# Self-attention of all batches as one stage, with its keys and queries in a ring, its sums turned by DMA, and the output projection in a second loop

## The reference

```
x   = L0(x, ctx_1024)                       # attention over 1601 rows of memory, a gate, RMS norm
n   = rms_norm(x, ln_in_w)
q,k,v = split(where(vm, n @ v_qkv, n @ l_qkv), 3)      # vm: which of two experts a token has
q,k = apply_rotary(heads(q,16,32), heads(k,16,32))
p   = softmax(causal(q * 32**-0.5 @ k.T))              # 16 heads, 512 x 512
ctx = p @ v
h   = x + where(vm, ctx @ v_dense, ctx @ l_dense)
h   = h + cross_attention(rms_norm(h), ctx_1024) @ cdense_w
out = h + where(vm, ffn_v(rms_norm(h)), ffn_l(rms_norm(h)))
```

## Time and profile before

| what | us |
| --- | --- |
| median of three runs | 2756.47 (2754.41 to 2765.78) |
| the profiled execution | 2762.2 |
| its span | 2760.1 |
| mean granted clock of TensorE | 0.863 of 2.4 GHz |
| the loop over batches, first product to the start of cross-attention | 39.3 to 1609.7 |

### The profile page before, as it was taken

The page is one execution under the profiler, slowest core; times in us unless marked ns, Lnnn a source line. Parts: engine busy times, 40 slices in busy tenths (PEclk is TensorE's granted clock), DMA queues, the critical chain, the costliest instruction groups (busy, mean ns, idle before and its releaser), DMA issues. The chain is left out here.

```text
span 2760.1 us, 35393 instructions
## 1 busy us (share of the span) xinstructions
PE 2270.3 (82%) x13534; PEld 1459.8 (53%) x13534; DVE 1598.8 (58%) x2420; ACT 937.4 (34%) x1627; POOL 394.5 (14%) x412
## 2 busy tenths in 40 slices
PE   5996776868758869659868649999999979999968
PEld 3673454654545745446634523444444357787846
DVE  4284433564423664442854458999999446666534
ACT  1131231221132212131312206888888822212101
POOL 0120001120002110002100000222222312221111
PEclk8986787976868967779868758999999989999989
DMA  4024044141062250261240392444444023343332
GB/s 151 24 75 101 13 96 157 47 106 48 16 165 85 66 132 3 70 179 31 77 107 1 83 171 44 82 82 82 82 85 91 15 83 91 102 115 86 100 84 72
DMA packets 196269, 227.89 MB, mean 83 GB/s; under 512 B 54134, under 2 KB 128250, under 8 KB 195306
## 3 DMA queue, kind: packets, MB, share of 16 engines
q1 hardware_dynamic: 189132, 217.98, 32.1%
q0 software_dynamic: 6656, 6.96, 1.0%
q10 hardware_dynamic: 288, 0.27, 0.0%
HBM read 162.76 MB, written 34.98 MB: 72 GB/s over the span
## 5 line engine op out<-in xcount | busy, mean ns | idle before, releaser
L1430 DVE TENSOR_REDUCE quarters<-ps 128x2 f32<-128x804 f32 x512 | 483.2, 991 | 52.4 <-PE ps L1464 50.8
L1395 ACT ACTIVATE pT_x<-ps 128x512 f32<-128x512 f32 (+1 forms) x832 | 451.6, 595 | 104.3 <-PE ps L1492 77.2
L184 DVE TENSOR_TENSOR w_lo<-w_raw,w_hi 128x512 fp32r<-128x512 f32 (+2 forms) x357 | 276.0, 773 | 12.2
L182 DVE CAST w_hi<-w_raw 128x512 fp32r<-128x512 f32 (+2 forms) x357 | 177.6, 498 | 181.9 <-PE ps L190 106.3
L1464 PE MATMUL ps<-kx_ring,qx_ring 63*128 63x402 f32 x1024 | 234.4, 470 | 45.7 <-DMA kx_ring<-cross_k_by_part 33.9
L1507 PE MATMUL ps<-pT_x,vx_ring 128*17 128x256 f32 (+1 forms) x3328 | 261.9, 388 | 0.2 <-ACT osb_x L1377 0.2
L1464 PEld LDWEIGHTS ps<-kx_ring,qx_ring 63*128 63x128 f32 x1024 | 100.4, 193 | 238.6 <-DVE quarters L1430 123.5
L877 ACT ACTIVATE pT_s<-ps 128x1024 f32<-128x1024 f32 (+3 forms) x128 | 88.8, 704 | 359.2 <-PE ps L963 359.2
L188 PE MATMUL ps<-mi_h,w_hi 128*128 128x512 f32 (+1 forms) x440 | 175.2, 398 | 37.4 <-issue 25.6
L894 DVE TENSOR_REDUCE row_max_s<-ps 128x1 f32<-128x128 f32 (+3 forms) x256 | 123.8, 491 | 137.9 <-PE ps L933 133.9
L1492 PE MATMUL ps<-qx_ring,kx_ring 64*128 64x512 f32 (+1 forms) x832 | 175.1, 417 | 6.2 <-ACT pT_x L1395 2.6
(11 more groups left out here) (273 smaller groups left out, 4512.3 us busy)
## 6 DMA issues: line engine op xcount, KB each, us to landing
kx_ring<-cross_k_by_part SPq DMA_DIRECT2D x96, 200.2 KB, 7.2
w_raw<-L_xattn_l_qkv SPq DMA_DIRECT2D x48, 256.0 KB, 3.0
w_raw<-L_xattn_v_qkv SPq DMA_DIRECT2D x48, 256.0 KB, 2.7
w_raw<-L_xattn_l_gate SPq DMA_DIRECT2D x40, 256.0 KB, 2.9
w_raw<-L_xattn_l_up SPq DMA_DIRECT2D x40, 256.0 KB, 2.9
w_raw<-L_xattn_l_down SPq DMA_DIRECT2D x40, 256.0 KB, 2.7
q_st<-early SPq DMA_DIRECT2D x32, 256.0 KB, 5.2
cross_v_by_group<-v_aug SPq DMA_DIRECT2D x16, 442.0 KB
```

The lines of the kernel that those rows point to most:

```text
L182: nc.vector.tensor_copy(hi, raw).then_inc(s_high, 1)
L184: nc.vector.tensor_tensor(out=lo, in0=raw, in1=hi.bitcast(f32), op=ALU.subtract).then_inc(s_split, 1)
L1395: nc.scalar.activation(pT[0:kn, u % 3, j, :], ps[0:kn, 5 + v % 3, :], ACT.Exp, scale=SCALE)\
L1430: nc.vector.tensor_reduce(out=quarters[:, g % 2, pair, :, q, quarter], in_=ps[:, at:at + 2, 0:MAXW], axis=AX.X, op=ALU.max)\
```

## The change

`gate_qkv` now stores the high and low parts of the queries and keys, the values, the stream `h` and the flag `early_v` to DRAM, and the first loop ends there. Then `self_attention` runs once, for 16 groups. SP loads each group into one of four slots of a ring, six DMAs of 32 partitions and one of values; the slot of group g is free for loading when the scores of group g-4 are done. A score product is one head and one key tile in one of three banks, each with its own exponential. The maxima have three banks too. The sums, their reciprocals and the shift go by way of DRAM with DMAs that POOL issues; POOL divides, and stores the rows. A second loop runs `add_projection`, which loads the rows, the two masks, the flag, the weights and `h` back, masks on DVE, rounds on ACT and subtracts on POOL, and then `cross_projections`.

```diff
+    qs_d, ks_d = scratch("self_q_by_part", [B, 2, D, S]), scratch("self_k_by_part", [B, 2, D, S])
+    vs_d = scratch("self_v_by_group", [B, NH // 4, P, ST, P])
+    att_d = scratch("self_rows_by_batch", [B, P, NH // 4, S])
+    gated_d = scratch("stream_after_gate", [B, P, DT, S])
+    early_d = scratch("early_v_by_batch", [B, 1, 1], i32)
     keep_d = scratch("keep_expert_by_token", [2, B, S])
...
+                                sp.dma_start(keep_d[:, b, :].rearrange("e (a n) -> a e n", a=1), keep_expert[0:1, :, :])\
+                                    .then_inc(s["s_up"], 16)
+                                sp.dma_start(early_d[b], early_v[:, :]).then_inc(s["s_up"], 16)
+                        sp.wait_ge(s["s_h"], DT)
+                        sp.dma_start(gated_d[b], h[:, :, :]).then_inc(s["s_up"], 16)
+                        for c in range(2 * DT):
+                            dst, k = qs_d if c < DT else ks_d, c % DT
+                            for part, rows, ready in ((0, hi, "s_rh"), (1, lo, "s_rl")):
+                                sp.wait_ge(s[ready], c + 1)
+                                sp.dma_start(dst[b, part, k * P:(k + 1) * P, :], rows[c].bitcast(f32)).then_inc(s["s_up"], 16)
+                        sp.wait_ge(s["s_vn"], ST)
+                        for g in range(NH // 4):
+                            sp.dma_start(vs_d[b, g], v_nat[:, :, g * P:(g + 1) * P]).then_inc(s["s_up"], 16)
+                        sp.wait_ge(s["s_up"], 16 * (3 + 4 * DT + NH // 4))
 
                     @block.scalar
...
             first = maxima + 1 + lead
-            start, queue, by_step = queue[:first], queue[first:], []
-            for u in range(groups * steps):
-                g, kt = divmod(u, steps)
-                now = [(("flip", "back")[kt], g - 1)] if kt < 2 and g else []
-                due = -(-(u + 1) * (maxima + 1) // steps)
-                while queue and len(start) + sum(o[0] in ("max", "turn") for d in by_step + [now] for o in d) < first + due:
-                    now.append(queue.pop(0))
+            start, feed, given, by_step = feed[:first], feed[first:], 0, []
+            for v in range(groups * steps):
+                g, i = divmod(v, steps)
+                now = [("flip", g - 1)] if g and i == 11 else []
+                due = -(-(v + 1) * (maxima + 1) // steps)
+                while feed and given < due:
+                    now.append(feed.pop(0))
+                    given += 1
                 by_step.append(now)
...
                 with nc.Block() as block:
                     @block.sync
                     def _(sp):
-                        stack_heads(sp, k_st, (late[0].bitcast(f32), late[1].bitcast(f32), late[0].bitcast(f32)), HALF, HALF, 0, s["s_late"])
-                        preload(sp, next_tiles, s_pre)
+                        sp.dma_start(k_r[STACK:STACK + 1, :, :].bitcast(f32).rearrange("a (r h) n -> a r (h n)", r=8),
+                                     ones_d[:, 0:RING * 4 // 8 * S].rearrange("(a r) n -> a r n", a=1)).then_inc(s["s_one"], 16)
                         for g in range(NG):
-                            sp.wait_ge(s["s_used"], place["turn", g] + 1)
+                            b, i, rows = g // GB, g % RING, slice(g % GB * P, (g % GB + 1) * P)
+                            if g >= RING:
+                                sp.wait_ge(s["s_sc"], NU * (g - RING + 1))
+                            for ring, src, parts in ((q_r, qs_d, (0, 0, 1)), (k_r, ks_d, (0, 1, 0))):
+                                for r, part in enumerate(parts):
+                                    sp.dma_start(ring[r * HD:(r + 1) * HD, 4 * i:4 * i + 4, :].bitcast(f32),
+                                                 src[b, part, rows, :].rearrange("(j d) n -> d j n", d=HD)).then_inc(s_kq[i], 16)
+                            if g >= RING:
+                                sp.wait_ge(s["s_pv"], ST * (g - RING + 1))
+                            sp.dma_start(v_r[:, i, :, :], vs_d[b, g % GB]).then_inc(s_vr[i], 16)
...
+                    @block.gpsimd
+                    def _(pool):
+                        def shifts(g):
+
+                            pool.wait_ge(s["s_used"], place["turn", g] + 1)
+                            pool.dma_start(shift_d[g % 2], shift[:, g % 2, :].bitcast(f32)).then_inc(s["s_so"], 16)
+                            pool.wait_ge(s["s_so"], 16 * (g + 1))
+                            i = g % RING
+                            pool.dma_start(q_r[STACK:STACK + 1, 4 * i:4 * i + 4, :].bitcast(f32),
+                                           shift_d[g % 2].rearrange("(o j q) n -> o j (q n)", o=1, q=ST)).then_inc(s["s_sh"], 16)
+
+                        def spread_sums(g):
+
+                            pool.wait_ge(s["s_ob"], g + 1)
+                            pool.dma_start(sums_d[g % 2], osb[0:P:HD, g % 2, 1, :]).then_inc(s["s_ro"], 16)
+                            pool.wait_ge(s["s_ro"], 16 * (2 * g + 1))
+                            if g:
+                                pool.wait_ge(s["s_rq"], g)
+                            pool.dma_start(sums[:, :], sums_d[g % 2].rearrange("j (c n) -> (j c) n", n=4 * ST)).then_inc(s["s_rs"], 16)
+
+                        def scale_rows(g):
+
+                            pool.wait_ge(s["s_rq"], g + 1)
+                            pool.dma_start(inverse_d[g % 2], rq[:, :]).then_inc(s["s_ro"], 16)
+                            pool.wait_ge(s["s_ro"], 16 * (2 * g + 2))
+                            if g:
+                                pool.wait_ge(s["s_at"], g)
                             for j in range(4):
-                                sp.dma_start(q_st[3 * HD:3 * HD + 1, 4 * g + j, :].bitcast(f32),
-                                             shift[j:j + 1, g, :].bitcast(f32)).then_inc(s["s_sh"], 16)
+                                pool.dma_start(rq_rows[j * HD:(j + 1) * HD, :],
+                                               inverse_d[g % 2, j * HD:(j + 1) * HD, :].rearrange("(o c) n -> o (c n)", o=1)
+                                               .broadcast_to((HD, S))).then_inc(s["s_rb"], 16)
+                            pool.wait_ge(s["s_rb"], 64 * (g + 1))
+                            if g >= 2:
+                                pool.wait_ge(s["s_up"], 16 * (g - 1))
+                            nc.gpsimd.tensor_tensor(out=att[:, g % 2, :], in0=osb[:, g % 2, 0, :], in1=rq_rows[:, :], op=ALU.mult)\
+                                .then_inc(s["s_at"], 1)
+                            pool.wait_ge(s["s_at"], g + 1)
+                            pool.dma_start(att_d[g // GB, :, g % GB, :], att[:, g % 2, :]).then_inc(s["s_up"], 16)
+
+                        shifts(0)
+                        for g in range(NG):
+                            if g:
+                                spread_sums(g - 1)
+                            if g + 1 < NG:
+                                shifts(g + 1)
+                            if g:
+                                scale_rows(g - 1)
+                        spread_sums(NG - 1)
+                        scale_rows(NG - 1)
+                        pool.wait_ge(s["s_up"], 16 * NG)
...
+                        def keep_sums(g):
+
+                            act.wait_ge(s["s_pv"], ST * (g + 1))
+                            if g >= 2:
+                                act.wait_ge(s["s_at"], g - 1)
+                            nc.scalar.activation(osb[:, g % 2, :, :], ps[:, VALUES:SUMS + 1, :], ACT.Copy).then_inc(s["s_ob"], 1)
...
+                                pe.wait_ge(s["s_used"], place["max", g, len(max_units) - 1] + 1)
+                                last = nc.tensor.matmul(bank[0:4 * ST, 0:P],
+                                                        row_max[:, g % 2, :, :].rearrange("p j q -> p (j q)"), neg_ident[:, :],
+                                                        start=True, stop=True)
...
+                            g, i = divmod(v, NU)
+                            kt, j, heads = score_units[i]
+                            width, cut, at = S - kt * P, slice(kt * P, (kt + 1) * P), 4 * (g % RING) + j
+                            bank = ps[:, SCORES + v % 3, :]
+                            if v == 0:
+                                pe.wait_ge(s["s_one"], 16)
+                            if i == 0:
+                                pe.wait_ge(s["s_sh"], 16 * (g + 1))
+                            if v >= 3:
+                                pe.wait_ge(s["s_exp"], v - 2)
...
+                        for v in range(NG * NU):
+                            todo = [o for o in by_step[v] if o in place]
+                            if v + 2 < NG * NU:
+                                scores(v + 2)
+                            if todo:
                                 fill(todo.pop(0))
...
+                        for k in range(DT):
+                            sp.dma_start(att[:, k, :], att_d[b, :, k, :]).then_inc(s["s_att"], 16)
+                            if k == 0:
```

(52 more changed lines are left out.)

313 lines of the change are left out of this document (131 added, 182 removed).

## The result

The changed kernel takes **2732.9 us** (median of 4 runs, 2730.9 to 2738.6) beside 2757.0 for the kernel before (4 runs, 2754.4 to 2765.8): ratio 0.991, 95% interval 0.9884 to 0.9937. It is faster by 24 us. I had predicted 2653, within 2605 to 2728: the sign is right, the gain is a quarter of the 104 us forecast, and the time lies 5 us above the range. The profiled execution took 2738.6 (span 2736.8) against 2762.2 before, so it shows the same 24 us, and 81 us more than the 2658 that my sum gave by its measure.

What follows compares the result with a forecast made beforehand. The prediction took PE, partly at half clock and partly waiting, to bound the kernel. Self-attention -134, gate -25, new border +34, projection +41, cross border -23, barrier +3 make -104: 2653 us, range 2605 to 2728.

Steps and rivals of the forecast that it cites:

- the period: Self-attention: time X per group, from PE's work W and its stall s before the shift; taken as 16.0 us.
- POOL's quiet list, 13.0: Self-attention: POOL's serial transfers and division for one group, at quiet transfer times, take 13.0 us.
- PE's own work, 13.7: Self-attention: PE's scores, maxima, values and turn for one group at full clock take 13.7 us.
- The burst, 8 us: Self-attention: one group's ring loads of queries, keys and values take 8 us, bounds 5.8 and 12.4.
- Which transfers meet the burst: Self-attention: POOL's four row loads land with the ring loads, 8 us; later sums and shift run quiet, 6.5 us.
- The clock: Self-attention: a 1.5 us stall every period can lower PE's clock; W of 14 to 15.4 gives 15.4 to 16.1.
- Rival 1: Self-attention: POOL's transfers hardly wait for ring loads, period 13.7 us, whole kernel 2610 us; chance 0.22.
- (a): Gate's end: stores ride along with the rotation, so it ends at 223.7 instead of 229.9 us; -25 us in all.
- (b): New border from gate to memory, 10.3 us; three of these and one plain barrier with the loop's end, +34 us.
- (c): Second loop's projection: loads come first, first product at 10.7 us, stage 34.5 instead of 24.3 us; +41 us in all.
- rival 2: Self-attention: ring loads run at the slow end, 12.4 us, period 18.3 us, whole kernel 2698 us; chance 0.15.
- rival 4: Self-attention: each burst holds up POOL for its whole length, period 25.4 us, whole kernel about 2800 us; chance 0.05.

Runs made afterwards that it cites:

- e1: Changed kernel without SyncE's ring loads of groups 4 to 15 of self-attention, which compute on the data of groups 0 to 3; 2656.3 us.
- e2: Changed kernel with both transfers of the shift issued by SyncE ahead of the ring loads of its turn, not by POOL; 2703.3 us.
- e6: Changed kernel with the shift on SyncE ahead of the loads, and POOL's list reordered so sums leave before the division of the group before; 2676.3 us.
- e12: Changed kernel with paced loads, shift on SyncE among them, POOL's list reordered, reciprocal after 15 units, projection subtracting on DVE and waiting per tile pair; 2629.5 us.
- e10: e6 with the burst of ring loads issued about half a group later, when the sums of the group before have landed; 2683.1 us.
- e9: e6 with DVE taking the reciprocal after 15 of the 16 units of a group instead of 11; 2678.5 us.
- e7: Changed kernel with the six ring loads of queries and keys issued one for every two scores instead of all together; 2701.9 us.

## Why the prediction was wrong

**The step that failed** is the period: "X = 8 + 2.3 + 6.5 - s, and PE gives X = W + s, so X = (16.8 + W)/2", with "I take 16.0". It measured 20.5, and 15 x 4.5 is 68 of the 81 us missed. Its terms one by one:

- *POOL's quiet list, 13.0.* Nearly right for the quiet tail, 13.3 (1143.4 to 1156.7 us), but 14.2 in e1, where the list runs beside a busy PE without any ring load.
- *PE's own work, 13.7.* 0.7 short (14.4 in e1, e2, e6 and e12). So the "0.7 us to spare" of the list were 0.2.
- *The burst, 8 us.* Somewhat short: its six loads land 9.1 us after the first is issued at 932.8, and with the values 10.8 us after 918.4, within the stated bounds of 5.8 and 12.4. The formula makes X longer by half of the 1.1 to 2.8 us: 0.6 to 1.4 of the 4.5 missed.
- *Which transfers meet the burst.* This is the fault. I put the four row loads behind the burst and let "the list goes on: 2.3 us to the end of the store, then 2.03 + 0.57 + 1.97 + 1.9", all quiet. The formula assumes that the order in time of burst and list is the same in every period. But the list was then so late that the next burst met its shift and its inverse, 5 us more. Those are outside the formula, and so is the beat of two groups.
- *The clock.* "W between 14 and 15.4" held for a stall of 1.5 us. With stops of 9 us PE's work was 17.3 a group at a mean of 0.78. I had the mechanism, but put into it a stall from the term that failed. With W = 17.3 and a burst of 9.1 to 10.8 us the formula would give 17.6 to 18.5; what is left up to 20.5 is what it leaves out.
- *Rival 1's rule.* Under bursts POOL's transfers did wait, 4 to 7 us for what takes 1.4 to 2. The Trainium skill's page "DMA: Bandwidth & Descriptors" (section SWDGE vs HWDGE vs iDMA) has the queues served in turn; that small transfers would pass the loads by it, as the rival had it, is not borne out by these rows. Where the loads are spread, in e12, the shift's store landed in 1.4 to 3.5 us; that one is on SyncE's own queue.

**The other steps.** "First scores at 33", with 5 for the clock: 35.6, right. "The last group without maxima 10, and its division 15": 34 together, since POOL had another group's division in front. Borders (a) and (b): right, 3 us better than the sum in all four batches together. (c), the projection at 34.5: 36.9 to 38.0, its first product at 13.3 instead of 10.7 in the second batch. That the ring loads are hidden, since "a group's maxima begin 1.7 groups ahead of its scores": right, PE waits for no ring load in the changed kernel; e10 shows how near that is.

**The rivals.** The measured 20.5 lies between rival 2 (18.3, slow loads) and rival 4 (25.4, "every burst of loads holds up POOL for its whole length"). What happens is rival 4 in a milder form, about 5 us of a burst of 9 to 11 us in every group; with 0.05 I had it too low. My argument against it, that only one of four trips stood in the way in the earlier trace rows, took a kernel whose POOL had nothing late for evidence about one whose POOL is. No rival had the second hook, the reciprocal, although the text named it; e2, e6 and e9 show it to be the next stop as soon as the shift is on time.

**What stays open.** Why each change alone gives 22 to 31 us and the combination 90 is argued from the stops, not shown part by part. The nearest pair is e9 and e12. They differ in self-attention only in the pacing of the loads and in the shift's place among them, and the second loop begins at 1126.3 us in e9 and at 1096.4 in e12, 30 us earlier; the first exponentials are at 832.7 and 832.3, so the first shift has no part in it. How much of the 30 is the pacing and how much the shift's place was not separated. Nor does a run tell why POOL's list takes 14.2 us in e1 and 13.3 in the tail.

## What to carry to other kernels

A serial chain of small transfers that just fits into a period has to be priced with the burst in front of each link in turn, and over several periods, until the pattern repeats: one link held up shifts the next ones into the next burst. Large prefetches that have a whole period of time are issued one at a time through it, not all when the slot comes free; small transfers with a deadline go into the same list between them. When a wait is removed and little comes back, read in the new trace which instruction now stands at the head of the in-order queue (here the reciprocal ahead of five maxima).

## What the runs showed of the hardware

- POOL waited 1.4 to 2.0 us for a transfer of 8 KB in the changed kernel's tail, with no ring load under way, and up to 3.2 in e1, also without one. It waited up to 4.4 next to single loads of 256 KB (e7), and behind a burst of six up to 5.6 in the changed kernel and 6.9 in e10. For the four of 64 KB it was 1.7, up to 3.4 next to single loads (e12) and up to 7.4 behind a burst.
- The first shift, issued by POOL at 827 us among the initial loads (a mean of 201 GB/s from 800 to 842 us), took 7.3 us out and as much in; in e2, on SyncE and behind two groups' loads only, it brought the first exponential from 842.9 to 834.5 us.
- With one stop of 9 us in a pair of groups the mean granted clock over the pair was 0.78. Around the stop from 933.1 to 942.1 us it was 1.00 from 910.7, 0.50 from 934.6 and 1.00 again from 955.1. With no stops it was 1.00 for 120 us on end (e1 and e12). The 22 us of such a group are 14.4 of work at full clock, 2.9 more for the lower clock and 4.7 of stop.
